# Buffers of C and of dt of a selective scan moved six words off the grid of 16 words

## The reference, cut to what matters

```
def ssm_direction(u, x_proj_w, dt_w, dt_b, A_log, D_skip):
    proj = u @ x_proj_w
    dt = softplus(proj[..., :DT_RANK] @ dt_w + dt_b)
    Bm, Cm = proj[..., DT_RANK:DT_RANK + 16], proj[..., DT_RANK + 16:]
    # per step: h = exp(dt * A) * h + (dt * u) * B ;  y = sum over states of h * C
    return selective_scan(u, dt, -exp(A_log), Bm, Cm) + u * D_skip
y = layernorm(merge_w[0] * y_forward + merge_w[1] * y_backward) * silu(z)
out = y @ W_out + residual
```

## Time and profile before

| | us |
|---|---|
| three runs, median (lowest, highest) | 1049.5 (1047.43, 1049.77) |
| the profiled execution's own time | 1040.84 |
| its span in the profile | 1039.1 |
| VectorE busy | 737.8 (71%) |
| TensorE busy | 764.9 (74%) |
| ScalarE busy | 708.7 (68%) |
| GpSimd busy | 649.2 (62%) |

### The profile page before, as it was taken

The page is one execution under the profiler, slowest core; times in us unless marked ns, Lnnn a source line. Parts: engine busy times, 40 slices in busy tenths (PEclk is TensorE's granted clock), DMA queues, the critical chain, the costliest instruction groups (busy, mean ns, idle before and its releaser), DMA issues. The chain is left out here.

```text
span 1039.1 us, 14980 instructions
## 1 busy us (share of the span) xinstructions
PE 764.9 (74%) x5308; PEld 665.1 (64%) x5309; DVE 737.8 (71%) x836; ACT 708.7 (68%) x1189; POOL 649.2 (62%) x359
## 2 busy tenths in 40 slices
PE   0559772787878778789887888656626887999991
PEld 0225321677777777678776877556525877999991
DVE  4898387899999999999999999964155111222224
ACT  0134895999999999899998999324242444565652
POOL 7435555699998999799998999602113656221120
PEclk9969665899999999999999999986655899899996
DMA  4012101112123112212111222299986752000005
GB/s 85 0 61 121 66 26 28 55 61 82 62 81 123 61 65 79 82 62 76 68 62 70 73 82 81 78 314 211 258 188 149 144 129 60 24 19 23 19 23 190
DMA packets 31902, 91.92 MB, mean 88 GB/s; under 512 B 7560, under 2 KB 15264, under 8 KB 30824
## 3 DMA queue, kind: packets, MB, share of 16 engines
q1 hardware_dynamic: 20792, 57.53, 16.4%
q0 software_dynamic: 8352, 27.07, 12.1%
q10 hardware_dynamic: 2704, 6.61, 1.9%
HBM read 77.67 MB, written 13.53 MB: 88 GB/s over the span
## 5 line engine op out<-in xcount | busy, mean ns | idle before, releaser
L1376 PE MATMUL ps<-ident,arena 128*128 128x128 f32 (+1 forms) x3390 | 433.3, 282 | 171.6 <-DVE arena L818 54.7
L1376 PEld LDWEIGHTS ps<-ident,arena 128*128 128x128 f32 (+1 forms) x3390 | 381.0, 144 | 218.4 <-DVE arena L818 70.2
L559 POOL TENSOR_TENSOR arena<-arena 128x1024 f32<-128x1024 f32 x192 | 426.7, 2248 | 44.0 <-DVE arena L818 41.6
L818 DVE TENSOR_TENSOR_SCAN arena<-arena,ps 128x1024 f32<-128x1024 f32 x192 | 428.0, 2271 | 5.0 <-PE ps L1376 3.6
L1206 ACT ACTIVATE arena<-arena,neg_a 128x510 f32<-128x510 f32 x384 | 241.4, 714 | 0.0
L1192 ACT ACTIVATE arena<-arena 128x384 f32<-128x384 f32 x224 | 116.8, 607 | 9.0 <-PE ps L1376 8.9
L1192 ACT ACTIVATE arena<-ln_in,arena 128x384 f32<-128x384 f32 x224 | 116.8, 609 | 5.5 <-PE ps L1376 5.4
L1035 DVE TENSOR_SCALAR ln_in<-ps 128x768 f32<-128x768 f32 x39 | 37.3, 957 | 112.4 <-PE ps L1619 82.0
L618 POOL DMA_INDIRECT y_rows<-arena x39 | 37.9, 971 | 115.1 <-DVE arena L1040 107.6
L1629 PE MATMUL ps<-arena,ln_in 128*128 x468 | 85.4, 332 | 9.8 <-issue 7.2
L1629 PEld LDWEIGHTS ps<-arena,ln_in 128*128 128x128 f32 x468 | 76.9, 194 | 10.5 <-issue 10.4
(11 more groups left out here) (206 smaller groups left out, 830.0 us busy)
## 6 DMA issues: line engine op xcount, KB each, us to landing
arena<-b_rows SPq DMA_DIRECT2D x64, 512.0 KB, 3.5
arena<-ws SPq DMA_DIRECT2D x16, 576.0 KB, 9.3
arena<-wf POOLq DMA_DIRECT2D x16, 576.0 KB
arena<-hf POOLq DMA_DIRECT2D x16, 576.0 KB
gates_dram<-arena SPq DMA_DIRECT2D x4, 1536.0 KB, 5.1
arena<-gates_dram ACTq DMA_DIRECT2D x3, 1536.0 KB, 12.9
arena<-y_rows SPq DMA_DIRECT2D x4, 768.0 KB, 7.2
arena<-gates_dram SPq DMA_DIRECT2D x1, 1536.0 KB, 8.8
```

What stands on the lines that cost most here:

```text
L559: g_.tensor_tensor(state[i % STATES], state[i % STATES], c_bc[u % C_BUFS], ALU.mult).then_inc(s_mul, 1)
L818: v.tensor_tensor_scan(o, a, x, 0.0, ALU.mult, ALU.add).then_inc(s_scan, 1)
L1376: return mm(o, src, ident[at:at + parts, at:at + parts], start=start, stop=True, is_transpose=True, skip_group_check=True)
```

## The change

It adds unused words ahead of two sets of buffers, and fills up to the next 16 behind them. Starts within the arena shift: `dt_all` by 6 words, `bt` and the buffers cut behind it by 16, `c_bc[1]` and `c_bc[2]` by 22, and decay, state, dtu and c_bc[0] by 32. `temps` is set behind the first skew, so the buffers that begin there shift by 6. No instruction is added, removed or moved.

```diff
+SKEW, LINE = 6, 16
...
         u_all = [cut([DB, GT]) for _ in range(NG)]
         y_all = [m.rearrange("p a b -> p (a b)").rearrange("p (t d) -> p t d", d=DI) for m in u_all]
+        used[0] += SKEW
         temps = used[0]
         dt_all = [[cut([DB, GT]) for _ in range(2)] for _ in range(NG)]
+        used[0] += LINE - SKEW
         bt = cut([TILES, 2 * NS])
         fronts = used[0]
 
+        used[0] += SKEW
         c_bc = [None] + [cut([PAIR, GT]) for _ in range(C_BUFS - 1)]
+        used[0] += LINE - SKEW
         decay = [[cut([PAIR, GT]) for _ in range(DB)] for _ in range(2)]
         state = [cut([PAIR, GT]) for _ in range(STATES)]
```

## The result

Twenty runs of each gave a median of 1041.69 us (1039.91 to 1047.61) against 1047.91 (1044.2 to 1049.88) for the kernel before: ratio 0.9948, 95% interval 0.9937 to 0.9960, or 4.2 to 6.6 us less. Faster, as forecast, but by some 5.4 us where the text said 3.7 (the medians themselves differ by 6.2), and the median lies under the range given, 1042.5 to 1049.6. The profiled execution of the changed kernel took 1042.31 (span 1040.6), *more* than the 1040.84 of the profile before. Up to the start of the last scan it is 5.1 us ahead; from there to the end it takes 382.9 us where the profile before took 376.3.

What follows compares the result with a forecast made beforehand. VectorE was taken to set the scan stage's pace, with GpSimd nearly as full. Terms of -2.8 (scan stage) and -0.9 (before it) gave -3.7 us, from 1049.5 to 1045.8, range 1042.5 to 1049.6.

Steps and rivals of the forecast that it cites:

- GpSimd's durations: GpSimd operations with moved inputs: all 192 multiplies by C near 2.00 us, L548 near 2.89, L538 near 2.86.
- The scan stage, -2.8: From 186.4 to 668 us: VectorE's five gaps after the products of dt and u go, 2.8 us less.
- The multiplies alone give back 2.2 of the 2.78: Scan stage: faster multiplies with C buffers 1 and 2 recover 2.2 of the 2.78 us of VectorE's gaps.
- The replay: Group 1's stretch around L548 recomputed with faster multiplies: L548 starts at 339.6, not 339.96; 1.3 of 1.48 us comes back.
- dt: Scan stage: with dt moved and u not, L548 takes 2.89 us, 0.57 less, more than the 0.3 left of any gap.
- the upper bound: Scan stage: at most 3.9 us gained, the five gaps with the start-up wait of 1.11 besides.
- Before the scan, -0.9: Before the scan stage: shorter L538 shortens VectorE's waits, 0.57 at L647 and 0.30 of two others reaching the end.
- Only the inputs' order: Rival, chance 0.17: only L559's input order is cured, L538 and L548 stay at 3.45; 1047.3 us.
- ScalarE late next: Rival, chance 0.13: ScalarE's lead is too thin in the scan stage, half the scan gain left; 1047.2 to 1048.5 us.
- VectorE pays: Rival, chance 0.08: VectorE's L779 and L787 slow down on inputs that lie apart; up to +9, 1054.8 us.
- The change does not do what it says: Rival, chance 0.08: distance in the arena, not the offset, made buffer 0 fast, so nothing happens; 1049.5 us.
- The lock falls the other way: Rival, chance 0.04: at 60.5 us VectorE's L647 goes before GpSimd's L538, 3.4 us off its path; 1042.5 us.

Runs made afterwards that it cites:

- e4: Changed kernel with the gain and bias buffer also moved six words, so both inputs of gate_in's multiply lie equally off the grid; 0.9946 of the kernel before.
- e7: Changed kernel with decay, state and all cut behind them moved by the same six words as C; 0.9964 of the kernel before.
- e8: Kernel before with only C buffer 0 moved onto the grid, where buffers 1 and 2 are; 1.0051 of the kernel before.
- e6: Kernel before, no buffer moved, the product of dt and u ahead of unit 4 of groups 0 to 2 cut to one block of three; 0.9943.
- e2: Changed kernel with only C buffers 1 and 2 still moved, dt, conv, sz and gate_in back on the grid; 0.9954 of the kernel before.
- e5: Changed kernel, unchanged, run again on another chip; 0.9940 of the kernel before.
- e18: Changed kernel with sp_w six words off the grid and resid six words from ln_in's offset; 0.9879 of the kernel before.
- e9: Kernel before with C buffers at distances 2, 4 and 8 words; one run for durations, multiply medians 2.000, 2.371 and 2.378 us.
- e10: Kernel before with C buffers at distances 1, 12 and 14 words; one run for durations, multiply medians 2.000, 2.370 and 1.998 us.

## Why the prediction was right and wrong

**GpSimd's durations: right.** 2.00 for all 192, 2.91 where 2.89 was forecast and 2.90 where 2.86 was. The rule that the two inputs must lie apart, read from one operation with both durations, held in four more, the subtraction and the norm's sum among them; e4, e7 and e8 turned it around. What counts in it is a step of 4 words, not the 16 of my grid. By the Trainium skill's floor for two inputs (GPSIMD Engine Reference, Instruction dispatch), about 2.5 cycles an element, nothing should go below my estimate of 2.13; 192 rows stand at 2.00, and the rows decide.

**The scan stage, -2.8: this is the step that failed.** The mechanism was right (e6: with the product short, the gaps go and the gain is there); the size was not. The stage gives 3.8 in the first profile and 5.4 on average. Two things were wrong with "I take 2.8, the measured gaps". First, the idle time printed before an instruction is less than what it is late: scans that follow each other start 2.17 to 2.20 us apart while each record is 2.27 long, so records overlap by 0.07 and more, and a scan late by 0.15 shows no idle time. By starts, the same profile gives 3.8. Second, a gap was taken as a constant. In four of five profiles the granted clock is at its lower level behind one to three of TensorE's waits, the transposes that VectorE waits for take longer (40 in 6.25 us), and the excess is 5.1 to 7.1. What makes the clock fall in one execution and not in the next stays open; one profile could not show that it does.

**"The multiplies alone give back 2.2 of the 2.78": too little.** They give back all (e2). The replay made one multiply ahead of the product shorter, 0.36 us; but all three of unit 19 are slow and GpSimd is already behind when it takes the product up, so that it starts 0.75 earlier, which covers the 0.2 that the replay had left over. With *dt* after it, the sum came out at the whole of the gaps all the same. And the upper bound, with the start-up wait of 1.11 in it, counted something that comes and goes without the change.

**Before the scan, -0.9: not shown to arrive.** L652 gave its 0.5 in the changed kernel, and in that kernel's first profile the last product starts 0.65 earlier; in its second (e5) it starts 1.3 later than in the first profile of before. Between the two lie 12 products of TensorE that take 7.3 to 8.8 us according to the granted clock (from 66 to 74 us it is 0.70 in the first profile of before, with 7.52; 0.67 in the first of the changed kernel, with 8.10; 0.60 in e5, with 8.78), and this spread is more than the gain.

**The base.** The forecast stood on a median of three, 1049.5; of twenty it is 1047.91. That, 1.6 us, and the 2.6 by which the scan stage gave more make up the miss of 4.1 against 1041.69, if the 0.9 arrived; without it, 3.3 of it, and the rest is within what the medians can tell. Set on the forecast's own base, the measured ratio would give 1044.0, inside the range: that the median fell under it is in part the luck of the first three runs. The 5.4 against 3.7 is not, since the interval begins at 4.2.

**The rivals.** *Only the inputs' order* fell: 2.90 and 2.91. *ScalarE late next* fell: no gap is left behind the products. *VectorE pays* fell: 1751/1752/1758. *The change does not do what it says* fell with the second mode in the result, and its reason, the far place of buffer 0, with e8. *The lock falls the other way* did not happen here, and did in e18.

## What to carry to other kernels

An engine with idle time to spare can still set the pace: what counts is how fast it catches up behind its longest operation (the number of buffers between it and the next engine should matter too; no run here varied it). Look for operations of one shape with two durations, and ask what differs in where their operands lie. And take the size of a gap from the starts of several profiles, not from the idle time printed in one: where TensorE is in the loop, its clock can be part of the gap.

## What the runs showed of the hardware

A GpSimd operation on two float32 inputs takes 1.95 ns an element if the inputs' addresses differ by 1, 2, 6 or 14 words, and 2.32 if by 0, 4, 8 or 12 (2.00 and 2.37 us per 1024), at each place of the pair that was tried. Per 1536 elements it is 2.90 against 3.42 to 3.47. Four words are 16 bytes; the Trainium skill, SBUF — State Buffer, section Specifications, gives that as the size of a line of the memory. The step of four words in e9 and e10 agrees with that size; that this is why was not tried. VectorE's sum of two float32 inputs into dt shows no such effect: 1.75 us per 1536 at distance 0 and at 6.
